# Batch 0 of a fused adaLN block: low parts of the output weights on VectorE, query chunks loaded first, half tiles of the output projection inside attention

## What is computed

```python
h = _layernorm(x) * (1 + ca) + sa
q = (h @ wq).reshape(B, S, 32, 128); k = (h @ wk).reshape(B, S, 8, 128); v = (h @ wv).reshape(B, S, 8, 128)
q, k = _rope(q, pos), _rope(k, pos)
scores = einsum('bqhgd,bshd->bhgqs', qg, k) * 128 ** -0.5     # masked to j <= i and j > i - 256
out = einsum('bhgqs,bshd->bqhgd', softmax(scores), v).reshape(B, S, 4096)
x = x + ga * (out @ wo)
x = x + gb * lora_experts(_layernorm(x) * (1 + cb) + sb)
```

## Time and profile before

| | us |
|---|---|
| median of 3 runs | 2682.35 (2678.28 to 2682.72) |
| profiled execution | 2682.8 |
| its span (first to last instruction) | 2681.0 |
| TensorE busy | 2611.1 (97%) |
| VectorE busy | 1595.7 (60%) |
| ScalarE busy | 1155.1 (43%) |
| GpSimd busy | 249.5 (9%) |
| DMA, mean over the span | 186 GB/s |

### The profile page before, as it was taken

One profiled execution on the slowest core, in us unless ns is written; L12 is line 12 of the kernel. 1 busy time (PEld: TensorE's weight loads), 2 busy tenths in 40 slices (PEclk: granted clock), 3 DMA queues, 4 the chain that ended last, 5 costly groups with the idle time before them and its releaser, 6 DMA issues.

```text
span 2681.0 us, 40311 instructions
## 1 busy us (share of the span) xinstructions
PE 2611.1 (97%) x12873; PEld 2156.4 (80%) x12873; DVE 1595.7 (60%) x4151; ACT 1155.1 (43%) x2582; POOL 249.5 (9%) x120
## 2 busy tenths in 40 slices
PE   5999999999999999999999999999999999998999
PEld 3777787888888888888888888888888887776887
DVE  3767666666766655556665665556666665446553
ACT  3555554554344443333454443333444443325441
POOL 2323333231000000000000000000000000000122
PEclk8999999999999999999999999999999999999999
DMA  7667765558555443446445454336455455536221
GB/s 285 259 213 250 258 216 194 199 197 310 218 180 180 145 143 136 156 156 244 163 166 180 172 181 157 125 144 257 181 196 205 179 188 212 205 126 242 104 79 55
DMA packets 175640, 499.78 MB, mean 186 GB/s; under 512 B 15088, under 2 KB 57392, under 8 KB 174000
## 3 DMA queue, kind: packets, MB, share of 16 engines
q1 hardware_dynamic: 170352, 479.61, 49.6%
q10 hardware_dynamic: 5184, 18.88, 1.8%
HBM read 376.76 MB, written 121.67 MB: 186 GB/s over the span
## 4 chain that ended last, share of the span: by engine, by line
PE 75%; issue 15%; POOL 5%; DMA 2%; DVE 1%; ACT 1%; SPq 0%; ACTq 0%; POOLq 0%; DVEq 0%
PE bank L635 23%; PE bank L637 23%; PE bank L636 23%; PE bank L700 4%; POOL w_q_lo L605 3%; POOL w_o_lo L605 2%; DMA stage<-in_wmod 1%; DMA stage<-in_wv 1%; POOL w_k_lo L605 1%; PE bank L1643 0%; PE bank L248 0%; DVE rotated L1055 0%; PE bank L728 0%; POOL w_v_lo L605 0%; DMA wm<-in_wmod 0%
## 5 line engine op out<-in xcount | busy, mean ns | idle before, releaser
L635 PE MATMUL bank<-w_o_hi,qo_hi 128*128 128x512 f32 x1024 | 409.5, 400 | 0.9 <-DVE acc L1072 0.7
L635 PE MATMUL bank<-hT_hi,w_q_hi 128*128 128x512 f32 x1024 | 403.8, 394 | 0.2 <-DVE swapped L1052 0.2
L637 PE MATMUL bank<-w_o_hi,qo_lo 128*128 128x512 f32 x1024 | 399.9, 391 | 0.0
L637 PE MATMUL bank<-hT_hi,w_q_lo 128*128 128x512 f32 x1024 | 399.5, 390 | 0.0
L636 PE MATMUL bank<-hT_lo,w_q_hi 128*128 128x512 f32 x1024 | 399.5, 390 | 0.0
L636 PE MATMUL bank<-w_o_lo,qo_hi 128*128 128x512 f32 x1024 | 398.9, 390 | 0.0
L879 ACT ACTIVATE prob<-prob,nbias 128x384 f32<-128x384 f32 (+2 forms) x512 | 273.6, 534 | 130.7 <-DVE nbias L1085 117.1
L1085 DVE CUSTOM_DVE_ANT_0 prob<-bank,mask_t 128x384 f32<-128x384 f32 (+2 forms) x512 | 231.6, 454 | 144.1 <-PE bank L637 91.2
L1051 DVE TENSOR_TENSOR rotated<-bank,cos_t 128x512 f32<-128x512 f32 x160 | 110.7, 692 | 323.9 <-ACT swapped L863 321.6
L956 ACT ACTIVATE pT_hi<-bank 128x384 fp32r<-128x384 f32 (+2 forms) x512 | 204.1, 405 | 184.9 <-PE bank L700 179.7
L1072 DVE TENSOR_TENSOR acc<-bank,acc 128x512 f32<-128x512 f32 x256 | 173.9, 689 | 184.0 <-PE bank L637 184.0
(11 more groups left out here) (195 smaller groups left out, 4770.9 us busy)
## 6 DMA issues: line engine op xcount, KB each, us to landing
w_q_hi<-w_q_hi_scratch SPq DMA_DIRECT2D x96, 512.0 KB, 8.3
w_q_lo<-w_q_lo_scratch SPq DMA_DIRECT2D x96, 512.0 KB, 8.9
w_o_hi<-w_o_hi_scratch SPq DMA_DIRECT2D x96, 512.0 KB, 8.1
w_o_lo<-w_o_lo_scratch SPq DMA_DIRECT2D x96, 512.0 KB, 8.6
stage<-in_wq SPq DMA_DIRECT2D x32, 512.0 KB, 5.5
stage<-in_wo SPq DMA_DIRECT2D x32, 512.0 KB, 5.3
w_q_hi_scratch<-w_q_hi SPq DMA_DIRECT2D x32, 512.0 KB, 6.5
w_q_lo_scratch<-w_q_lo SPq DMA_DIRECT2D x32, 512.0 KB, 7.3
```

The source lines that it names most:

```text
L635: eng.matmul(o, st[0], mv_[0], start=start, stop=False)
L637: return eng.matmul(o, st[1], mv_[0], start=False, stop=stop)
```

## The change

Only batch 0 (the groups that split raw weights) changes its work:

- The low parts of the four output-weight chunks are computed by VectorE (`dve_chunk`, semaphore `s_osplit`), not GpSimd: chunks 6, 7 and 8 inside ropes 1, 2 and 3, chunk 9 ahead of rope 4. GpSimd keeps six chunks.
- Chunks are numbered anew: 0 to 3 Q, 4 V, 5 K. Chunks 0 and 1 of the next group are copied by ScalarE at the tail of attention.
- SP's queue issues a chunk's load and behind it the stores of the chunk four back, and of chunks 6 and 7 after chunk 9's load.
- TensorE's and VectorE's order in batch 0 becomes that of the other batches: four half tiles of the output projection inside attention, K at units 0 to 7, and V in the first group as in all others.
- ScalarE's columns of the layer-norm tile are spread as 2, 4 and 2.

```diff
         def sp_chunk(eng, n, j):
-            eng.wait_ge(s_split, 10 * n + j + 1)
+            if j < 2:
+                eng.wait_ge(s_osplit, 4 * n - 1 + j)
+            elif j < 8:
+                eng.wait_ge(s_split, 6 * n + j + 1)
+            else:
+                eng.wait_ge(s_osplit, 4 * n + j - 7)
             load_chunk(eng, (1 + j) % 2, j, (n + 1) % KV if j == 5 else n % KV)
...
+        def sp_split_group(eng, n, before_q=lambda: None):
+            def keep(j):
+                sp_keep(eng, j, (n + 1) % KV if j == 5 else n)
+            for j in range(2):
+                sp_chunk(eng, n, j)
+                sp_keep(eng, NC - 2 + j, n - 1)
+            before_q()
+            for j in range(2, NC):
+                sp_chunk(eng, n, j)
+                if j >= 4:
+                    keep(j - 4)
+            for j in (NC - 4, NC - 3):
+                keep(j)
...
             for t in range(QT):
-                n = 1 + t
-                for j in range(NC):
-                    if j == 2:
-                        sp_tile_load(eng, n, x_tile(0, t))
-                    sp_chunk(eng, n, j)
-                    jj, nn = (NC - 2 + j, n - 1) if j < 2 else (j - 2, n)
-                    sp_keep(eng, jj, (nn + 1) % KV if jj == 5 else nn)
+                sp_split_group(eng, 1 + t, lambda: sp_tile_load(eng, 1 + t, x_tile(0, t)))
                 sp_tile_store(eng, 0, t)
...
+        def dve_chunk(eng, n, j):
+            slot, dst, src = chunk(j)
+            eng.wait_ge(s_hi, 10 * n + j + 2)
+            eng.tensor_tensor(dst[1], src, dst[0].bitcast(F32), ALU.subtract).then_inc(s_osplit, 1)
...
         def p1_pool(eng):
             first_chunk(eng, True)
-            for j in range(NC):
+            for j in range(6):
                 pool_chunk(eng, 0, j)
             eng.wait_ge(s_mm1, KT)
             plain(eng.memset(acc[:], 0.0)).then_inc(s_acc0, 1)
...
         def p1_pe(eng):
             last = BATCH - 1
-            with eng.Fori(1, 1 + QT) as n:
-                pe_attention(eng, n - 1, K_SPLIT, False, False, o_direct=False)
-                for half in range(1, 8):
-                    pe_wo(eng, n - 1, half, False, False)
-                pe_qv(eng, n, False, n - 1)
-                eng.wait_ge(s_laf, n + 1)
...
+            pe_groups(eng, 0, True, False)
...
-        def act_project_split(eng, n, tile=None):
+        def act_first_chunks(eng, n):
             for j in (0, 1):
                 act_chunk(eng, n, j)
+
+        def act_project_split(eng, n, tile=None):
             act_rope(eng, n, 0, True)
             act_chunk(eng, n, 2)
+            act_chunk(eng, n, 3)
             if tile is not None:
                 act_tile_sqrt(eng, tile)
-            for j in (3, 4, 5):
-                act_chunk(eng, n, j)
-            for r in range(1, 1 + GQ):
+            act_chunk(eng, n, 4)
+            act_chunk(eng, n, 5)
...
+            act_rope(eng, n, 1, True, lambda: act_tile(eng, tile, range(0, 2)))
+            act_tile(eng, tile, range(2, 6))
+            act_rope(eng, n, 2, True, lambda: act_tile(eng, tile, range(6, KT)))
+            act_tile_hi(eng, tile)
+            for r in (3, 4):
                 act_rope(eng, n, r, True)
-                if r <= 2 and tile is not None:
-                    act_tile(eng, tile, range(4 * (r - 1), 4 * r))
-            if tile is not None:
-                eng.wait_ge(s_hst, 32 * (tile + 1))
+            eng.wait_ge(s_hst, 32 * (tile + 1))
...
         def dve_rope(eng, n, r, split=False):
             if r == GQ:
                 for u in range(EARLY):
                     dve_mask(eng, n, u)
+                if split:
+                    dve_chunk(eng, n, NC - 1)
...
-            between()
+            if split and 1 <= r < GQ:
+                dve_chunk(eng, n, 5 + r)
             eng.wait_ge(s_rh, 5 * n + r + 1)
             eng.wait_ge(s_ra, 5 * n + r + 1)
```

More of the change, by code:

```diff
@@ L173, in p0_act @@
             for r in range(1, 1 + GQ):
[L174 to L176 removed]
+                act_rope(eng, 0, r, True)
         def sp_store_gate(eng, q, row):
@@ L232, in p0_dve @@
             for r in range(1 + GQ):
-                dve_rope(eng, 0, r, False)
+                if r == GQ:
+                    eng.wait_ge(s_md[0], 64)
+                dve_rope(eng, 0, r, split=True)
                 if r == 2:
                     dve_late_gate(eng, 0, mrow[:], mabs[:], msgn[:])
[L236 to L242, removed]
         def pe_slice(eng, i, rows):
@@ L302, in p0_pe @@
                 pe_project(eng, 0, f"Q{h}", w_q, slice(h * HD, (h + 1) * HD), 1 - h % 2, {}, gate)
[L303 to L306, removed]
+            pe_v(eng, 0, False)
         p1 = ExitStack()
@@ L590, in act_chunk @@
             slot, dst, src = chunk(j)
-            if j == 0:
+            first = isinstance(n, int) and n == 0
+            if j == 0 and not first:
+                eng.wait_ge(s_proj, 6 * n)
+            elif j == 4:
                 eng.wait_ge(s_proj, 6 * n + 1)
@@ L596, in act_chunk @@
                 eng.wait_ge(s_wo, 8 * n + 1)
-            if not (isinstance(n, int) and n == 0):
+            if not first:
                 eng.wait_ge(s_ws[j], 32 * n)
@@ L657, in pe_tile, with wo_bank, pe_wo @@
             m.then_inc(s_lt, 1)
-        def wo_bank(half, fill):
-            return bank[1] if fill and half < FILL else SBANK[half % 3]
-        def pe_wo(eng, n, half, fill, direct):
+        def wo_bank(half):
+            return bank[1] if half < FILL else SBANK[half % 3]
+        def pe_wo(eng, n, half, direct):
             t, c = divmod(half, 2)
@@ L745, in pe_attention @@
                     pe_values(eng, n, u // GQ - 1)
-                if fill and u in WO_AT:
-                    pe_wo(eng, n, WO_AT.index(u), True, o_direct)
-            if not fill:
-                pe_wo(eng, n, 0, False, o_direct)
+                if u in WO_AT:
+                    pe_wo(eng, n, WO_AT.index(u), o_direct)
             pe_values(eng, n, QT - 1)
@@ L865, in act_rope @@
                 act_chunk(eng, n, 5 + r)
-            if r == GQ and early:
+            if r == GQ:
                 for u in range(EARLY):
                     act_exp(eng, n, u)
+            between()
             dst = kt_[0][:] if r == 0 else qo[0][:, r - 1, :]
@@ L1041, in adaln_block, with dve_rope @@
         LN_VAR = 3 * QT + 1
-        def dve_rope(eng, n, r, early=True, between=lambda: None):
+        def dve_rope(eng, n, r, split=False):
             slot = r % 2
             bk = bank[0 if r % 2 == 0 else 1]
-            if r == GQ and early:
+            if r == GQ:
                 for u in range(EARLY):
                     dve_mask(eng, n, u)
+                if split:
+                    dve_chunk(eng, n, NC - 1)
             eng.wait_ge(s_proj, 6 * n + 2 + r)
@@ L1071, in dve_wo @@
             a = acc[:, t, cc * 512:(cc + 1) * 512]
-            eng.tensor_tensor(a, wo_bank(half, fill)[:], a, ALU.add).then_inc(s_wor, 1)
+            eng.tensor_tensor(a, wo_bank(half)[:], a, ALU.add).then_inc(s_wor, 1)
         def dve_outputs(eng, n, i):
@@ L1097, in adaln_block, with dve_attention @@
         WO_SUM = (12, 14, 16)
-        def dve_attention(eng, n, b, last=False, fill=True):
+        def dve_attention(eng, n, b, last=False):
             for s in range(EARLY + 1, UNITS + LAG):
-                if fill and s in WO_SUM:
+                if s in WO_SUM:
                     if s == WO_SUM[0]:
@@ L1126, in dve_attention @@
                     dve_last(eng, s)
-                if fill and s == UNITS + LAG - 1:
+                if s == UNITS + LAG - 1:
                     dve_wo(eng, n, FILL - 1)
@@ L1256, in p1_dve, with dve_group @@
             dve_groups(eng, last, False)
-        def dve_group(eng, n, b, part=None):
+        def dve_group(eng, n, b, part=None, split=False):
             dve_attention(eng, n - 1, b)
@@ L1290, in dve_groups @@
                         dve_tile_lo(eng, i)
-                    dve_rope(eng, n, r)
+                    dve_rope(eng, n, r, split)
                     if not ln and r in (2, 3):
```

169 lines of the change are left out of this document (74 added, 95 removed).

## The result

| | before | after |
|---|---|---|
| median, us | 2682.35 | 2689.6 (2688.7 to 2693.69, 7 runs) |
| profiled execution, us | 2682.8 | 2692.78 |
| its span, us | 2681.0 | 2691.0 |
| GpSimd busy, us | 249.5 | 170.7 |

The ratio of after to before is 1.003, 95% interval 1.0021 to 1.004. The forecast was 2681.0, no change; the kernel became slower by 7.3 us, more than can be taken for no change, though inside the range of 2659 to 2694.

What follows compares the result with a forecast made beforehand. It took TensorE as the bound (75% of the chain, plus 15% issue). Prologue -4.5, tile groups +5.6, plain groups -5.8 and reload +3.5 sum to -1.2 us on 2682.35: 2681 us, range 2659 to 2694.

Steps and rivals of the forecast that it cites:

- the low clock: Half-rate TensorE clock after the new wait at V in each tile group: 1.3 us each.
- a group's own time: Batch-0 groups without new wait or low clock, priced by batch 1's 73.32 and 72.14 us plus 0.3.
- prologue: First group, second score to first turn of attention: 4.5 us gained, at most 5.0.
- wait for `hT`: End of batch 0: four more stores ahead of the reload put it 3.5 us later, bounds 0 and +5.
- The queue of stores: Tile groups: tile's store behind six weight stores lands at 50.2 us; TensorE waits 4.9 us at its turn of V.
- rival 1: Tile's store lands about in time, wait 0 to 2.5 us, no low clock: total 2655 to 2665; chance 0.25.
- the forecast's own sign: Test for batch 0's plain groups: if they stay over 73.5 us, the step on batch 1's periods was wrong.
- the step on batch 1's periods: TensorE's own time in batch-0 groups priced by batch 1's periods, 73.32 and 72.14 us, plus 0.3.
- Low parts on VectorE: Projection: four 1.23 us VectorE operations replace four 2.4 us on GpSimd; costed at 0.3 us a group.
- DMA at full share: Second queue test: 12.6 MB at 371 GB/s takes 34 us, so the tile lands near 48 to 50.
- Rival 3: Load chain becomes the bound, at Q3's start; each group loses 1.5 to 2 us more: 2692 to 2695; chance 0.17.
- Rival 4: Waits for `prob` stay for another reason, leaving only the queue's cost: 2688; chance 0.04.

Runs made afterwards that it cites:

- e1_store_first: The changed kernel with the layer-norm tile's two stores issued right behind chunk 9's load, ahead of the stores of chunks 5, 6 and 7: 2661.56 us, ratio 0.9919.
- e5_low_on_gpsimd: e1_store_first with the low parts of the four output-weight chunks computed by GpSimd again: 2690.97 us, ratio 1.0028.
- e3_reload_too: e1_store_first, plus in batch 0's last group the reload of `hT` ahead of the stores of chunks 7, 8 and 9: 2658.97 us, ratio 0.9908.
- e7_two_waits: e3_reload_too, with SP waiting for stores of chunks 0 to 5 before the first fetch, of 6 to 9 only before output weights: 2653.79 us, ratio 0.9896.
- e6_half_tiles_alone: The kernel before the change, with only the four half tiles and K moved inside batch 0's attention: 2730.42 us, ratio 1.0179.
- e2_store_mid: The changed kernel with the tile's stores behind those of chunks 5 and 6, ahead of chunk 7's only: 2677.69 us, ratio 0.9987.

## Why the prediction was wrong

Between the forecast of -1.2 us and the +9.3 us of the periods lie 10.5 us. Two terms of the sum were sized too small: the low clock, 6.0 us, and a group's own time, 6.4 us. The others give 1.9 back (prologue -1.4, waits at V 4 x -0.3 = -1.2, wait for `hT` +0.7). The mechanism, stores in the way of the tile's store, was forecast as it is.

**The queue of stores: right.** The forecast had chunk 9 at +34, the tile landed at +50.2 and a wait of 4.9 us at the turn of V; the trace has +35.1, +49.9 and 4.20 to 4.79. `e1_store_first` confirms the cause, and with it the gain that rival 1 spoke of: 2661.56 us, against its 2655 to 2665, though there the tile was to land in time by itself, and it did not.

**The low clock: the first step that failed.** The forecast took 1.3 us for it, read from behind a wait of 1.82 us, and put it behind a wait of 4.9. Measured behind 4.2 to 4.8 us it is 2.2 us in the mean. The same step left it out behind the reload of `hT`, where the wait alone was costed at 3.5 us: it was 4.21 us, but the period grew by 6.7, and the 2.5 us between are the low clock (0.50, 0.50 and 0.58 in three windows of 2 us). From that K product to the first half tile TensorE takes 7.91 us (643.62 to 651.53), the same matmuls before 5.15 (637.05 to 642.20). So (8.7 - 4 x 1.3) + 2.5 = 6.0 us are this term, 8.7 being the four prices at V. The plain groups carry a little of it too: a period is cut at `v__lo`, where the low clock still holds, and the first of the three is 74.45 us, the others 73.07 and 73.09.

**A group's own time: the second step that failed.** The forecast priced the seven groups without wait at V and clock at 4 x 73.62 + 3 x 72.44 = 511.8 us. The changed kernel takes 545.4 for them, less 18.4 for the four waits and 8.7 for the clock: 518.2, 6.4 us more. (`e1_store_first`, which has no wait at V, takes 516.2.) The plain price came from a period with 356 matmul records; one of 358 beside it takes 72.38, so 3 x 0.24 = 0.7 us is a badly picked row. The rest is what a group of batch 0 costs beyond one of batch 1. The forecast had 0.3 us a group for it, the price of the low parts on VectorE, with an upper bound of 1.2 for a whole chunk ahead of the first turn. Against batch 1's periods with as many matmuls the seven groups take 7.9 us more, 1.1 a group: 4.0 us are listed waits for VectorE, of 0.19 to 0.60 us, and 3.9 are not listed. In the second plain group they can be placed: beside the same matmuls of batch 1 TensorE loses nothing until the next attention's first turn, is 0.45 us late there (0.28 of it listed) and 0.68 at 560.77. VectorE, then TensorE:

```profile
555.80 1.22 DVE L623 TENSOR_TENSOR w_o_lo<-stage,w_o_hi 128x1024 fp32r<-128x1024 f32 x1 [1.86 <-ACT w_o_hi L612]
557.02 0.69 DVE L1075 TENSOR_TENSOR rotated<-bank,cos_t 128x512 f32<-128x512 f32 x1
...
559.28 0.47 DVE L1120 TENSOR_SCALAR prob<-prob,rrow 128x128 f32<-128x128 f32 x2
```
```profile
559.62 0.33 PE L715 MATMUL bank<-ident_t,prob 128*128 128x128 f32 x1 [0.28 <-DVE prob L1120]
```

VectorE waits for chunk 9's high part, makes its low part and only then begins rope 4, behind which it normalises the unit that the first turn needs. This is a reading of the trace; no run moves chunk 9 alone.

By the forecast's own sign the step on batch 1's periods fails too, if only just: the plain groups are 73.54 us in the mean, and 73.5 was the line.

**The prologue: right, and better.** From the second score (81.03) to the first turn (87.59) it now takes 6.56 us, 4.7 less than 11.24, where 4.5 was forecast; the wait of 3.43 us for `qo_lo` that stood at 86.20 is gone. The score itself comes 1.2 us earlier, which the forecast had left out.

**Low parts on VectorE: right in what they remove.** Not one of 35 sums is stretched. What the step saves was never costed by itself, since batch 1's periods stood for the whole. `e5_low_on_gpsimd` puts it at 29.4 us beside the other parts. The Trainium skill (SBUF — State Buffer, "SBUF: two separate sides") has VectorE and GpSimd share one port pair under an exclusive lock; by that rule the stretch should vanish where no GpSimd chunk is in flight, and the trace agrees: 694 ns at most for the sums, against 2899 before, and 1.17 us for the product at 141.74, where GpSimd works from 139.95 to 142.36.

**DMA at full share.** The prediction weighed the figure of 358 GB/s (the Trainium skill, DMA: Bandwidth & Descriptors, "Specifications") against the row of 371 GB/s, and the Trainium skill's figure would have put the tile's landing 1.2 us later than the row did. The trace agrees with the Trainium skill over the whole backlog and not over short stretches. From +14 to the landing the mean is 353 GB/s:

```profile
212.78:248.70 35.92, 33.10 (x157) 27.17 (x155) 22.05 (x42) 19.69 (x34) 6.88 (x3) 1.00 1.00 353
```

Over the last 14.8 us of it, from the load of chunk 9 on, it is 373 GB/s, and 422 in the window 250:252. So a rate read from a window of 3 us was too high for 34 us of work; the landing came 0.3 us before the forecast all the same, as that was counted from single landings.

**The rivals.** Rival 3 (the load chain as the bound, through the bank of the third query product) shows in its place but not in its size: four waits of 0.19 to 0.56 us, against 1.5 to 2 in each. Rival 4 fell: the waits for `prob` at the turns went from 21.1 us to 7.9. The line from the profile of the kernel before:

```profile
L700 PE MATMUL bank<-ident_t,prob 128*128 128x128 f32 x1152 | 206.9, 274 | 21.4 <-DVE prob L1095 21.1
```

**What stays open.** The unlisted 3.9 us were placed in one plain group only; and the differences of about 1 us between the same groups of `e3_reload_too` and `e7_two_waits` were not followed up.

## What to carry to other kernels

When stores are moved later in an in-order queue, ask for each store behind them who waits for it: here a 512 KB tile that an engine needs stood behind six that nobody needed soon, and moving it ahead of them turned a loss of 7 us into a gain of 21. Put work that the critical engine must wait for ahead of work that only fills the queue, and put small extra operations of a busy engine into a wait that it has anyway. And when a forecast adds a wait of TensorE, price the low clock behind it from several waits of about that length, at every place where such a wait is added.

## What was not expected of the hardware

How often the low clock came grew with the length of TensorE's wait ahead of it; its price did so at most in the mean. Behind waits of 1.80 to 1.94 us it came in some groups (2 of 4 before, 1.3 us each; 2 of 4 in `e6_half_tiles_alone`; 0 of 4 in `e5_low_on_gpsimd`), behind 1.73 to 2.15 us in 1 of 4 (`e2_store_mid`, 1.6 us), behind 2.23 and 2.57 us in both (`e5_low_on_gpsimd`), but not behind 2.91 us in `e3_reload_too`, where the windows behind the wait show the full clock:

```profile
666.00:668.00 2.00, 2.00 (x11) 1.64 (x10) 1.40 (x3) 1.18 (x2) 1.02 (x1) 1.00 0.00 0
```

Behind 3.2 us and more, in batch 0 of all these traces, it came every time, 17 of 17: seven in `e6_half_tiles_alone`, the wait of 3.43 us for `qo_lo` in the prologue there and before, four at V in the changed kernel, and four for `hT` at the reload.

The price behind waits of 4.2 to 4.8 us varied: 1.63 to 2.81 us at V, and at the reload, against 5.15 us for the same matmuls without it, 2.76 (wait 4.21, changed kernel), 2.18 (4.18, `e2_store_mid`), 2.46 (4.16, `e5_low_on_gpsimd`) and 1.44 us behind the longest wait there, 4.56 us in `e1_store_first`:

```profile
613.49 0.76 PE L651 MATMUL bank<-hT_hi,w_k_hi 128*128 128x512 f32 x1 [4.56 <-DMA hT_lo<-hT_lo_scratch]
...
620.08 0.47 PE L651 MATMUL bank<-w_o_hi,qo_hi 128*128 128x512 f32 x1
```

The mean of these eight is 2.2 us. What TensorE does between these waits differs, and no run changed the wait alone at one place over this whole range.
